# A Mamba block with a routed feed-forward on one core: the sort's counts taken on TensorE, two result buffers, and a new order of the work

## The chip, the core and the metric

The kernel runs on one core of a Trainium2 chip. The metric is the device time of one execution in microseconds (us). The kernel before was timed three times; the median is 2396.81 us.

## The reference

```python
x = x + mamba(layernorm(x))        # x: (8, 1024, 256) f32
    # mamba(x): xn = layernorm*g+b; u,z = split(xn @ W_in.T)   d_inner 512
    #   u = silu(conv4(u)+b);  dt,B,C = split(u @ W_xp.T)      16+16+16
    #   dt = softplus(dt @ W_dt.T + b_dt);  A = -exp(A_log)
    #   h = exp(dt*A)*h + (dt*u)*B;  y = sum_n h*C  + u*D      16 states
    #   return x + (y * silu(z)) @ W_out.T
x = x + moe(layernorm(x))
    # moe(x): logits = x @ router_w + router_b;  top 2 of 8 experts
    #   weights = softmax of the two logits; tokens sorted by expert
    #   out[token] += w * ((silu(x@gate_e) * (x@up_e)) @ down_e)
```

All is float32.

## The kernel before, in words

**Batches, slots, units.** The 8192 tokens are cut into NQ = 16 batches of T = 512. The scan over one batch is UN = 16 units: a unit is 32 channels x 4 states on the 128 partitions, J = 4 times over, 512 steps each. Time is laid out in slots. Each engine runs one Python loop over the slots and issues in each slot, in a fixed order, what falls there: unit s of the scan in slot s (batch q = s // 16, n = s % 16), besides it pieces of the front of the batches to come and of the tail of the batches before. The engines are tied by semaphores alone, so the order within a slot is the order of the queue and says nothing of time.

**One unit.** GpSimd's *drive* (L1301) writes the scan's input for four groups in one product; ScalarE's *decay* (L945) four exponentials; VectorE (L1089 to L1111) scans groups 0 and 1, multiplies both by C, scans 3, scans 2, multiplies 2; GpSimd's *weigh* (L1309) multiplies group 3; TensorE's *weigh* (L692) sums the states into `yps`. The buffer `hs` has three places, so the drive of unit u waits for TensorE's weigh of unit u-3 (`s_ymm`). GpSimd's slot s is: drive of unit s+1, other pieces, weigh of unit s.

**The front of a batch** is made on TensorE in one PSUM bank, `ring`: X (transposes), U and Z (in-projection), W (convolution), P (x-projection), D (dt), and for the tail O0, O1 (out-projection), F0, F1 (transposes), R0 (router), K0 (ranks). The tables MAKES (TensorE) and TAKES (ScalarE) give for each the slot, counted from the batch's first unit, and a place 0 to 4 within it. Since all but the first share one bank, a piece is made only when ScalarE has taken the piece made before it (`BEFORE`). SU and SZ are silu; D is followed by E (exponential, then two sums) on ScalarE, *round_off* (L1313) on GpSimd, L (logarithm, L886), then *less_lost*, *plus_relu* and *dtu* (L1319, L1324, L1329), which make softplus(dt) and dt*u; `pieces` gives their slots.

**The tail of a batch.** In slot 2 of the next batch VectorE takes the moments of the new x (L1062), GpSimd their deviation (L1273), ScalarE the normalised rows. In slot 7 `route` picks the top two experts (`gap` L1131, `hot` L1135), TensorE's `ranks` counts, for each token, the tokens before it with the same expert, and in slot 8 `weights` and `place` compute each token's row in a sorted copy in HBM. `scatter` (L1339) writes the rows there by indirect DMA from slot 8, one piece of 128 a slot (two a slot in the last two batches). Tiles of 128 sorted rows of one expert then pass through gate, up and down (`tile_transpose`, `gate_up`, `activate`, `down`) at the slots of TILE_AT; ScalarE copies the result into `yt` (L986), and `add_rows` (L1349) adds it into the output by an indirect DMA with addition, one at a time: each waits for the one before (`s_add`). The last batch has LAST = 22 tiles, placed TAIL_AT slots after its end; the tiles from slot LATE_FROM on (8 of batch 14 and these 22) run after the scan and take their weights from the arena.

**place() before.** `r5` holds the counts that `ranks` left in PSUM: for each of four groups of tokens the rank within the batch, and the batch's totals. `state[0]` is the next free row of each expert, `state[1]` the number of rows not yet given to a tile. 22 small VectorE instructions, most of which wait for the one before by `s_place`, form the positions, count full tiles, spread them over the batch's eight tile slots and leave `te` (expert) and `tb` (first row) for SyncE to load by.

## Time and profile before

| | us |
|---|---|
| three runs | 2390.99, 2396.81, 2398.17 |
| profiled execution, its own time | 2390.97 |
| its span | 2389.1 |
| granted TensorE clock, mean | 0.87 of full |
| VectorE busy | 1987.7 |
| GpSimd busy | 1957.3 |
| first drive starts | 75.5 |
| last drive starts | 2199.5 |

The span is from the first to the last instruction of the profiled execution; its time is 1.9 us more. Busy time is the time in which an engine runs an instruction, without its waits. The first and last drive mark where the scan begins and ends: before them lies the front of the first batch, behind them the tail.

### The profile page before, as it was taken

Reading aid. Unit: us, or ns where it says so; the run is one execution under the profiler, and the core shown is the slowest. Engines: PE = TensorE matmul, PEld = TensorE weight load, DVE = VectorE, ACT = ScalarE, POOL = GpSimd, SP = SyncE. Lnnn points to the kernel's source line nnn. Section 1 sums busy time; section 2 is a strip of 40 time slices with the busy share of each in tenths; the row PEclk is TensorE's granted clock in tenths of the full one; section 3 lists DMA queues with packets and bytes.
Section 4 is the critical chain, followed back from the end, with each engine's and each line's share of the span. In section 5 each row is a group of like instructions: output and inputs, shape, how many; then the busy total and the mean of one; then the engine's idle time right before and its main releaser. Section 6 shows DMA issues by size and latency. Waiting matters only on the chain.

```text
span 2389.1 us, 32277 instructions
## 1 busy us (share of the span) xinstructions
PE 1805.6 (76%) x7630; PEld 934.7 (39%) x7630; DVE 1987.7 (83%) x2756; ACT 1719.3 (72%) x3273; POOL 1957.3 (82%) x1284
## 2 busy tenths in 40 slices
PE   6557777686868788787968888786878878665885
PEld 2113222243434444443534444443534444243542
DVE  0499989999898989899898989999898989999311
ACT  5778677877887777877887677877878678754232
POOL 2688787979989897998989898998979898997333
PEclk9789788798989888897989889898989889777998
DMA  2545354575767676685758576686757667597332
GB/s 73 132 103 128 87 140 102 151 185 144 199 152 188 154 188 147 175 198 146 188 147 196 151 190 167 163 202 154 194 137 188 161 176 175 156 249 225 77 59 35
DMA packets 217979, 369.34 MB, mean 155 GB/s; under 512 B 31040, under 2 KB 86592, under 8 KB 217664
## 3 DMA queue, kind: packets, MB, share of 16 engines
q1 hardware_dynamic: 192208, 333.56, 54.0%
q0 software_dynamic: 25584, 33.71, 7.2%
q8 instruction: 65, 1.06, 0.2%
q14 instruction: 122, 1.00, 0.1%
HBM read 285.05 MB, written 83.01 MB: 154 GB/s over the span
## 4 chain that ended last, share of the span: by engine, by line
PE 35%; POOL 20%; issue 17%; ACT 16%; DVE 7%; DMA 4%; POOLq 0%; ACTq 0%; DVEq 0%
POOL arena L1301 7%; PE yps L692 5%; PE ring L594 4%; PE ring L602 4%; DMA out<-yt,xt 4%; PE p_g L724 4%; ACT dA L945 4%; DVE dA L1089 4%; PE ring L622 3%; POOL sorted_x L1339 3%; POOL arena L1309 2%; PE ring L610 2%; POOL out L1349 2%; POOL rst L1273 2%; PE p_a L704 2%
## 5 line engine op out<-in xcount | busy, mean ns | idle before, releaser
L1301 POOL TENSOR_TENSOR arena<-arena,b_bc 128x2048 f32<-128x2048 f32 x256 | 985.3, 3849 | 67.6 <-PE yps L692 63.7
L945 ACT ACTIVATE dA<-arena,a_s 128x512 f32<-128x512 f32 x1024 | 673.1, 683 | 135.7 <-DVE arena L1098 106.2
L1089 DVE TENSOR_TENSOR_SCAN dA<-dA,arena 128x512 f32<-128x512 f32 x384 | 454.7, 1215 | 137.7 <-ACT dA L945 103.1
L1089 DVE TENSOR_TENSOR_SCAN dA<-dA,carry,arena 128x512 f32<-128x512 f32 x384 | 477.8, 1275 | 39.2 <-POOL arena L1301 23.3
L692 PE MATMUL yps<-arena,const_s 128*32 128x512 f32 x2048 | 325.6, 712 | 210.8 <-POOL arena L1309 135.0
L1098 DVE TENSOR_TENSOR arena<-dA,c_bc 128x1024 f32<-128x1024 f32 x256 | 313.6, 1225 | 8.8
L1349 POOL DMA_INDIRECT out<-yt,xt x135 | 215.5, 1597 | 115.6 <-DMA out<-yt,xt 62.0
L1309 POOL TENSOR_TENSOR arena<-arena,c_bc 128x511 f32<-128x511 f32 (+1 forms) x256 | 296.0, 1156 | 15.7 <-DVE arena L1089 14.8
L594 PE MATMUL ring<-arena 128*128 128x512 f32 x488 | 258.6, 656 | 58.5 <-ACT arena L853 34.3
L724 PEld LDWEIGHTS p_g<-xT,w_e 128*128 128x128 f32 x1680 | 230.7, 215 | 28.9 <-issue 26.1
L724 PE MATMUL p_g<-xT,w_e 128*128 128x128 f32 x1680 | 236.1, 300 | 6.5 <-DVE hT L1222 6.5
L602 PE MATMUL ring<-arena 128*128 128x512 f32 x480 | 221.0, 603 | 19.9 <-ACT xn_t L928 9.6
L692 PEld LDWEIGHTS yps<-arena,const_s 128*32 128x32 f32 x2048 | 45.0, 117 | 395.2 <-issue 285.2
L1111 DVE TENSOR_TENSOR arena<-dA,c_bc 128x512 f32<-128x512 f32 x256 | 177.1, 692 | 8.3
L1339 POOL DMA_INDIRECT sorted_x<-xf,pos x128 | 128.0, 1000 | 47.1 <-issue 24.3
L1089 DVE TENSOR_TENSOR_SCAN arena<-dA,carry,arena 128x512 f32<-128x512 f32 x128 | 163.3, 1275 | 0.0
L594 PEld LDWEIGHTS ring<-arena 128*128 128x128 f32 x488 | 92.9, 207 | 171.1 <-issue 77.1
L1089 DVE TENSOR_TENSOR_SCAN arena<-dA,arena 128x512 f32<-128x512 f32 x128 | 155.3, 1214 | 0.3 <-ACT dA L945 0.3
L704 PE MATMUL p_a<-w_e,hT 128*128 128x256 f32 x420 | 146.3, 480 | 0.5 <-ACT xT L978 0.5
L1319 POOL TENSOR_TENSOR arena<-arena,t_s 128x512 f32<-128x512 f32 x64 | 80.6, 1260 | 70.9 <-ACT arena L886 70.5
L704 PEld LDWEIGHTS p_a<-w_e,hT 128*128 128x128 f32 x420 | 87.9, 232 | 129.9 <-issue 114.2
L602 PEld LDWEIGHTS ring<-arena 128*128 128x128 f32 x480 | 87.1, 191 | 122.3 <-issue 88.7
(165 smaller groups left out, 2967.6 us busy)
## 6 DMA issues: line engine op xcount, KB each, us to landing
arena<-dt_d SPq DMA_DIRECT2D x512, 256.0 KB
w_e<-in_w_moe SPq DMA_DIRECT2D x105, 512.0 KB
dt_d<-arena SPq DMA_DIRECT2D x128, 256.0 KB, 2.3
w_e<-in_w_moe SPq DMA_DIRECT2D x105, 256.0 KB
xt<-sorted_x SPq DMA_DIRECT2D x135, 129.0 KB
b_bc<-bc_d SPq DMA_DIRECT2D x256, 64.0 KB, 2.1
c_bc<-bc_d SPq DMA_DIRECT2D x256, 64.0 KB
xs<-in_x SPq DMA_DIRECT2D x16, 512.0 KB, 6.9
```

The source lines that it names most:

```text
L594: last = pe.matmul(bank(q, name), w_in_s[:, c, ch * P:(ch + 1) * P], xnT[:, c, :], start=c == 0, stop=c == DC - 1)
L602: last = pe.matmul(bank(q, f"W{c}"), d_conv[:, c, k, :], ubuf[:, c % 2, k:k + T], start=k == 0, stop=k == TAPS - 1)
L692: last = pe.matmul(yps[32 * j:32 * j + 32, :], sumsel, hs[:, u % 3, j, :], start=False, stop=g == G - 1, skip_group_check=True)
L704: last = pe.matmul(p_a[:, DM:2 * DM], hT[:, v % 2, c, :], w_e[:, v % 2, col:col + DM], start=c == 0, stop=c == DC - 1)
L724: last = pe.matmul(p_g[:, f, :], w_e[:, v % 2, col:col + P], xT[:, v % 2, c, :], start=c == 0, stop=c == DC - 1)
L945: act.activation(dA[:, j, :], rep_dt[:, c % 2, j, :], ACT.Exp, scale=a_s[:, n, j:j + 1]).then_inc(s_exp, 1)
L1089: return dve.tensor_tensor_scan(out_ap, dA[:, j, :], hs[:, u % 3, j, :], init, ALU.mult, ALU.add)
L1098: dve.tensor_tensor(hs[:, u % 3, 0:2], dA[:, 0:2], c_bc[:, g, :].unsqueeze(1).to_broadcast([P, 2, T]), ALU.mult).then_inc(s_m01, 1)
L1301: pool.tensor_tensor(hs[:, u % 3], rep_dtu[:, c % 2], b_bc[:, g, :].unsqueeze(1).to_broadcast([P, J, T]), ALU.mult).then_inc(s_dbu, 1)
L1309: pool.tensor_tensor(hs[:, u % 3, 3, 0:end], hs[:, u % 3, 3, 0:end], c_bc[:, g, 0:end], ALU.mult).then_inc(s_hp, 1)
L1339: pool.indirect_dma_start(out=sorted_x, out_offset=bass.IndirectOffsetOnAxis(ap=pos[:, q % 2, k, t:t + 1], axis=0), in_=xf[:, q % 2, t, :] ...
L1349: pool.indirect_dma_start(out=out_rows, out_offset=bass.IndirectOffsetOnAxis(ap=number, axis=0), in_=yt[:, v % NY, :], in_offset=None, bou ...
```

## The change

It has four parts.

1. `ranks` gets the running state into the sum on TensorE: two matmuls with the identity add `r5[:, QT]` (next free row) to all five rows and `r5[:, QT+1]` (rows not given out) to a sixth, and the counting matmuls run over one row more. `state` and `row` are gone: `r5` is [P, 6, 8] and is both the state and the new table. ScalarE's copy of it waits for `s_state` in place of `s_pos`.
2. `place` has 18 instructions for 22. `count_e`, `upto`, `some`, `base`, `step` and `past` are one or two columns wider, with borders set once at the start (three more memsets); the shifted copy of `upto`, the clipping of `te` and the last addition of `base` and row numbers are gone; `full` has a buffer of its own.
3. `yt` has two buffers for three (NY).
4. The order: MAKES, TAKES, `pieces`, `ahead`, the order of the calls in each engine's slot, SyncE's too, scatters two a slot for all batches, TAIL_AT 15 for 19.

```diff
-LG, PL, WT = 2, 16, 3
-NX, NY = 7, 3
+LG, PL, WT = 2, 13, 3
+NX, NY = 7, 2
-TAIL_AT = 19
+TAIL_AT = 15
-        a_slot = 2 if q >= NQ - 2 else 1
+        a_slot = 2 if q >= NQ - 2 else 2
...
 MAKES (slots and places that the prediction speaks of)
-  (-15,3) U2  (-14,2) U3  (-11,4) P0  (-10,4) D0  (-9,0) Z0  (-8,0) Z1
-  (16,4) O0   (17,4) O1   (1,0) D3    (21,1) R0   (23,2) K0
+  (-14,1) U2  (-14,4) U3  (-10,0) P0  (-10,2) D0  (-9,2) Z0  (-9,3) Z1
+  (16,3) O0   (17,1) O1   (1,0) D3    (21,2) R0   (23,3) K0
 TAKES
-  (-10,4) D0,E0  (-8,0) Z1,L0  (-3,2) L1  (0,3) L2  (17,0) O0  (23,3) K0
+  (-10,4) D0  (-9,0) E0  (-8,0) Z1,L0  (-3,2) L1  (0,0) L2  (17,2) O0  (24,0) K0
...
             def ranks(q):
+                pe.wait_ge(s_tables, 5)
+                wait(pe, s_state, q)
+                rows = ring[:, 0:(n + 2) * NE].rearrange("p (i e) -> p i e", e=NE)
+                pe.matmul(rows[:, 0:n + 1], ident, r5[:, n:n + 1, :].to_broadcast([P, n + 1, NE]), start=True, ...)
+                pe.matmul(rows[:, n + 1:n + 2], ident, r5[:, n + 1:n + 2, :], start=False, ...)
                 for k in range(2):
-                    pe.matmul(ring[:, 0:n * NE], before, hot[:, k, 0:n, :], start=k == 0, ...)
+                    pe.matmul(rows[:, 0:n], before, hot[:, k, 0:n, :], start=False, ...)
                     for i in range(n):
-                        later = n - i
+                        later = n + 1 - i
...
 TensorE's slot: weigh(s - 1) goes behind down, late_down and late_turn
 ScalarE's slot
-  keep01, decay 1, gap_exp, decay 0, second_weight, take 0, norm_x, decay 3, take 1, take 2, keep2,
-  norm_x2, take_y, take 3, decay 2, take_y (late), take 4, late_take, keep3, tanh, take_xt
+  second_weight, take 0, keep01, decay 0, norm_x, decay 1, decay 3, take 1, late_take, gap_exp, take 2,
+  norm_x2, keep2, keep3, take_y (late), take 3, take 4, decay 2, take_xt, tanh, take_y
 VectorE's slot: moments(0) first and a slot earlier, activate ahead of route
 GpSimd's slot
-  drive, add_rows, scatter, less_lost, plus_relu, dtu, deviation(0), round_off, weigh, deviation(1)
+  drive, deviation(0), add_rows, scatter, less_lost, weigh, deviation(1), plus_relu, dtu, round_off
-  plus_relu (-8, -2, 1, 3)  dtu (-7, -1, 1, 4)  round_off (-9, -3, -1, 2)
+  plus_relu (-8, -2, 0, 4)  dtu (-8, -2, 0, 4)  round_off (-9, -4, -1, 1)
 SyncE's slot
-  load_tile, store_bc (n 9), load_down, store_x2 (4), load_x (6), load_late, load_c, load_b,
-  store_dt (-6, -1, 2, 5), load_rep, load_expert
+  store_x2 (n 5), load_x (5), load_b, store_bc (6), load_down, load_tile, load_late,
+  store_dt (-5, 0, 3, 7), load_expert, load_rep, load_c
...
             def place(q):
-                a = row = r5[0:QT] + state[0]
-                c = row2 = hot * row
-                b = state += r5[QT]
-                d = full = state[1] >= 128, 256, ...
+                a = row2 = hot * r5[0:QT]
+                b = full = r5[QT + 1] >= 128, 256, ...
                 posf, count_e, pos, head, upto (scan)
-                past; upto[1] = upto[0] - count_e; base; some; step; tef; taken; past *= step
-                state[1] -= 128 * taken; tbf; te = min(tef, 7); tbf += base[0] + rows; tb = min(tbf, ZERO_PAGE)
+                past; base; some; step; tef; taken; past *= step
+                r5[QT + 1] -= 128 * taken; te = tef; tbf; tb = min(tbf, ZERO_PAGE)
```

In the tables, the two slot orders and `place` the diff is written out in short; a slot such as (-8, 0) is counted from the first unit of the batch, and 16 more or less is the same slot of a neighbouring batch.

## Rows read from the trace of the kernel before

**Rows 1.** The page: busy time by engine, and the chain by engine.
```profile
PE 1805.6 (76%) x7630; PEld 934.7 (39%) x7630; DVE 1987.7 (83%) x2756; ACT 1719.3 (72%) x3273; POOL 1957.3 (82%) x1284
...
PE 35%; POOL 20%; issue 17%; ACT 16%; DVE 7%; DMA 4%; POOLq 0%; ACTq 0%; DVEq 0%
```

**Rows 2.** Stretches: length, busy PE, PEld, DVE, ACT, POOL; PEclk, DMA share, GB/s.
```profile
75.50:2199.50 2124.00, 1627.04 (x7014) 833.43 (x7013) 1934.23 (x2608) 1621.22 (x3045) 1874.62 (x1198) 0.87 0.65 164
...
1140.00:1274.20 134.20, 107.59 (x497) 57.43 (x490) 121.41 (x171) 110.84 (x231) 121.63 (x79) 0.90 0.69 173
```

**Rows 3.** Waits of VectorE, 75 to 2199 us: us in total, times, longest.
```profile
DVE dA L1089 <- POOL arena L1301: 57.6, 64, 2.1
DVE stats L1062 <- ACT xs L924: 37.6, 14, 2.8
```

**Rows 4.** Waits of GpSimd, the same stretch.
```profile
POOL arena L1319 <- ACT arena L886: 69.6, 21, 6.2
POOL arena L1301 <- PE yps L692: 63.7, 21, 5.2
```

**Rows 5.** VectorE in time, batch 8, unit 2: start us, us, instruction, idle before.
```profile
1155.84 2.35 DVE L1089 TENSOR_TENSOR_SCAN dA<-dA,arena 128x512 f32<-128x512 f32 x2 [0.34 <-POOL arena L1301]
...
1162.29 0.69 DVE L1111 TENSOR_TENSOR arena<-dA,c_bc 128x512 f32<-128x512 f32 x1
1165.78 1.41 DVE L1062 BATCH_NORM_STATS2 stats<-xs 128x6 f32<-128x256 f32 x4 [2.80 <-ACT xs L924]
...
1167.52 2.31 DVE L1089 TENSOR_TENSOR_SCAN dA<-dA,arena 128x512 f32<-128x512 f32 x2
```

**Rows 6.** TensorE in time: the begin of O1; the begin of ranks.
```profile
1160.46 1.99 PE L622 MATMUL ring<-w_out_s,sz 128*128 128x256 f32 x8 [0.92 <-ACT arena L853]
...
1207.14 0.41 PE L647 MATMUL ring<-hot,const_s 128*128 128x32 f32 x2 [0.84 <-ACT sz L862]
```

**Rows 7.** ScalarE in time, batch 8, slots 7 and 8.
```profile
1209.58 0.20 ACT L934 ACTIVATE r<-ring 128x40 f32<-128x40 f32 x1 [2.07 <-PE ring L650]
...
1213.86 1.28 ACT L886 ACT_TABLE_LOAD   x1
1215.15 0.63 ACT L886 ACTIVATE arena<-arena 128x512 f32<-128x512 f32 x1
```

**Rows 8.** VectorE in time: the first and the last instruction of place().
```profile
1210.62 0.19 DVE L1167 TENSOR_TENSOR row<-r,state 128x32 f32<-128x32 f32 x1
...
1213.77 0.17 DVE L1210 TENSOR_SCALAR tb<-tbf 128x8 uint32<-128x8 f32 x1
```

**Rows 9.** GpSimd in time, batch 8: drive 8; slot 8.
```profile
1199.38 3.81 POOL L1301 TENSOR_TENSOR arena<-arena,b_bc 128x2048 f32<-128x2048 f32 x1 [3.45 <-PE yps L692]
...
1212.14 1.01 POOL L1339 DMA_INDIRECT sorted_x<-xf,pos  x1 [0.74 <-DVE pos L1182]
1215.86 1.08 POOL L1319 TENSOR_TENSOR arena<-arena,t_s 128x512 f32<-128x512 f32 x1 [2.71 <-ACT arena L886]
```

**Rows 10.** GpSimd's groups in batch 8: plus_relu and dtu; busy, mean ns, idle before.
```profile
L1324 POOL TENSOR_TENSOR arena<-arena 128x512 f32<-128x512 f32 x4 | 5.7, 1421 | 0.2
...
L1329 POOL TENSOR_TENSOR arena<-arena,uc 128x512 f32<-128x512 f32 x4 | 4.4, 1094 | 0.1
```

**Rows 11.** GpSimd in time: the first and the last of 22 additions.
```profile
2288.42 1.54 POOL L1349 DMA_INDIRECT out<-yt,xt  x1 [3.23 <-DMA out<-yt,xt]
...
2381.69 1.55 POOL L1349 DMA_INDIRECT out<-yt,xt  x1 [2.00 <-DMA out<-yt,xt]
```

**Rows 12.** Line 1131: shortest, median, longest ns; first and last start.
```profile
L1131 DVE TENSOR_TENSOR gap<-mx x16: 166/711/3484, 264.7 to 2247.4; 128x4 f32<-128x4 f32 x16
```

**Rows 13.** VectorE in time: line 1131 beside unit 7 of batches 8 and 15.
```profile
1203.80 1.08 DVE L1131 TENSOR_TENSOR gap<-mx 128x4 f32<-128x4 f32 x1
...
2147.34 3.48 DVE L1131 TENSOR_TENSOR gap<-mx 128x4 f32<-128x4 f32 x1
```

**Rows 14.** GpSimd in time, the same.
```profile
2147.00 3.81 POOL L1301 TENSOR_TENSOR arena<-arena,b_bc 128x2048 f32<-128x2048 f32 x1
```

More of the change, by code:

```diff
@@ L63, in __init__ @@
         elif q == NQ - 2:
-            self.at = [self.ready + k for k in [18, 20, 21, 22, 23, 25, 26, 28]]
+            self.at = [self.ready + k for k in [18, 20, 21, 22, 23, 25, 26, 29]]
         else:
@@ L261, in mamba_moe @@
         hot = sb("hot", [P, 2, QT, NE])
-        r5 = sb("r5", [P, QT + 1, NE])
-        state = sb("state", [P, 2, NE])
-        row = sb("row", [P, QT, NE])
+        r5 = sb("r5", [P, QT + 2, NE])
         row2 = sb("row2", [P, 2, QT, NE])
@@ L559, in _ @@
                         load_b(0, g)
-                for p, k in pieces(s, (-6, -1, 2, 5), (-10, -1, 3, 5)):
+                if q >= 0 and front and n == 6 or s == -13:
+                    store_bc(q + 1)
+                for g, k in tiles_in(s - 1, False):
+                    load_down(g, k)
+                for g, k in tiles_in(s + 1):
+                    load_tile(g, k)
+                if q == NQ - 1 and n in (4, 5, 6, 7, 9, 10, 13, 14):
+                    load_late((4, 5, 6, 7, 9, 10, 13, 14).index(n))
+                for p, k in pieces(s, (-5, 0, 3, 7), (-10, -1, 3, 7)):
                     store_dt(p, k)
+                for g, k in tiles_in(s + 1, False):
+                    load_expert(g, k)
                 if 0 <= q < NQ and n in (0, 4, 8):
@@ L575, in _ @@
                             no_tokens(e)
+                if n == 0 and 0 <= q < NQ:
+                    load_c(q, G - 1)
+                if front and n >= 13:
+                    load_c(q + 1, n - 13)
             sp.wait_ge(s_add, 16 * TILES)
@@ new lines, in place @@
+                h = step_of(dve.tensor_scalar(some[:], upto[:], float(nk), None, ALU.min))
+                dve.wait_ge(s_place, g5)
+                i = step_of(dve.tensor_tensor(step[:, 0:NE + 1], base[:, 1:NE + 2], base[:, 0:NE + 1], ALU.subtract))
+                dve.wait_ge(s_place, f)
+                dve.tensor_reduce(tef[:, 0:nk], past[:, 0:nk, 1:NE], AX_X, ALU.add).then_inc(s_past, 1)
+                dve.wait_ge(s_place, h)
+                j = step_of(dve.tensor_tensor(taken[:], some[:, 1:NE + 1], some[:, 0:NE], ALU.subtract))
@@ L1227, in _ @@
                 tail = 0 <= q - 1 < NQ
+                for p in ahead(s, 9, -21):
+                    moments(0, p)
                 if unit:
@@ L1237, in _ @@
                     unit_second(s)
+                for g, k in tiles_in(s - 2):
+                    activate(g, k)
                 if n == 7 and tail:
@@ L1243, in _ @@
                     moments(1, q - 1)
-                for p in ahead(s, 10, -21):
-                    moments(0, p)
                 if unit and n in (4, 8, 12):
@@ L1361, in _ @@
                     drive(s + 1)
+                for p in ahead(s, 11, -20):
+                    deviation(0, p)
                 for g, k in tiles_in(s - 4, False):
@@ L1369, in _ @@
                     less_lost(p, k)
-                for p, k in pieces(s, (-8, -2, 1, 3), (-11, -1, 1, 3)):
-                    plus_relu(p, k)
-                for p, k in pieces(s, (-7, -1, 1, 4), (-11, -1, 1, 4)):
-                    dtu(p, k)
-                for p in ahead(s, 11, -20):
-                    deviation(0, p)
-                for p, k in pieces(s, (-9, -3, -1, 2), (-12, -3, 0, 2)):
-                    round_off(p, k)
-                if s == UN * (NQ - 1) + 5:
-                    no_token()
                 if 0 <= s < UN * NQ:
@@ L1383, in _ @@
                     deviation(1, q - 1)
+                for p, k in pieces(s, (-8, -2, 0, 4), (-11, -1, 1, 4)):
+                    plus_relu(p, k)
+                if s == UN * (NQ - 1) + 6:
+                    no_token()
+                for p, k in pieces(s, (-8, -2, 0, 4), (-11, -1, 1, 4)):
+                    dtu(p, k)
+                for p, k in pieces(s, (-9, -4, -1, 1), (-12, -3, 0, 1)):
+                    round_off(p, k)
 def program(nc, args):
```

177 lines of the change are left out of this document (76 added, 101 removed), and 25 rows, old and new, of tables (MAKES, MAKES0, TAKES, TAKES0).

## The prediction

> **What bounds the kernel now.** I read the page's busy line and chain first [rows 1]. The reader is to see that no engine holds the path: VectorE is busy 83% of the span and GpSimd 82%, and the chain goes through all four. The stretches [rows 2] say where the time lies: 2124 of 2389 us between the first and the last drive of the scan's 256 units. In one batch (16 units, 134.2 us) VectorE works 121.4 us and GpSimd 121.6 us, so each is idle 12 to 13 us and neither can be sped up alone. The waits say at whose door this idle time lies. VectorE loses 57.6 us to GpSimd's drive and 37.6 us in 14 waits of the second layernorm's moments for ScalarE's copy of the out-projection [rows 3]. GpSimd loses 69.6 us to ScalarE's logarithm and 63.7 us to TensorE's weigh, which frees the buffer of the drive [rows 4].
>
> Within a batch the two take turns, which the timelines of batch 8 show. Unit 2 begins the moment its drive is there (0.34 us late) and unit 3 only 11.68 us later, where the moments sat idle for 2.80 us [rows 5]. In slots 4 to 8 GpSimd has little to do and waits for others; in slot 8 it waits 2.71 us for the logarithm, and ahead of drive 8 it waited 3.45 us for TensorE's weigh [rows 9]. From there to the next slot 2 it has no idle time to speak of, and VectorE follows it. So a batch is: GpSimd from the logarithm of slot 8 to drive 2, then VectorE from unit 2 to unit 8.
>
> **The change part by part.** The sum is made against the profiled execution (span 2389.1 us, its time 2391.0 us); the median of the runs is 5.8 us above it, and I add these at the end.
>
> 1. *Out-projection in slot 17, the moments' wait.* Before, O1 is made at place 4, behind U2: only when ScalarE has copied U2 (line 853), at 1160.46, can O1 begin; it lasts 4.6 us, so it ends when VectorE has long been done with unit 2 [rows 5, 6]. After, U2 is gone to slot 18 and O1 stands right behind D3. Against this, O0 is taken later in ScalarE's slot (place 2 for place 0), about 1.1 us, and D3 and O1 with it: O0 copied 1155.0, D3 made and taken 1157.4, O1 ends 1162.0, its copy 1162.7 (hand reckoning with the same durations), while unit 2 itself keeps VectorE until 1162.98. The wait goes whole. What is late next is drive 3: GpSimd has 9.0 us of work between drives 2 and 3 (a row addition, plus_relu, dtu, weigh, drive), and VectorE's unit 2 without the stall has 8.9, which would cover almost the whole gain at units 3 and 4 if nothing else moved. But plus_relu and dtu of slot 1 (1.42 + 1.09 us [rows 10]) go to slot 0, ahead of drive 2, so drive 3 is no longer in the way. Value: 14 waits, 37.6 us [rows 3], of which I take 36. Bounds 0 and 37.6.
>
> 2. *GpSimd's order and the scatters in pairs.* Its work in a batch stays as it is; it only moves. In front of the logarithm's wait in slot 8 there now stand two scatters for one: 1.0 us and a gap of 0.2 [rows 9] leave the loaded stretch. The logarithm itself comes earlier: ScalarE now takes K0, Z1 and L0 ahead of its own decays, so it waits for TensorE's ranks (end about 1210.0), Z1 (1.8 us), the copy, the table load and the logarithm (0.5 + 1.28 + 0.63 [rows 7]), about 1214.7 where it was 1215.8, 1.1 us. Against these two, the 2.5 us of plus_relu and dtu now ahead of drive 2. Net for drive 2: +0.2 us a batch, taken as 0. Bounds over 14 batches: -32 us (if the two pieces fill time that is idle) to +34 us (if neither of the gains comes).
>
> 3. *place(), 18 small steps for 22.* It runs from 1210.62 to 1213.94 [rows 8], 3.3 us, 0.15 each; the wider tables (10 columns for 8) cost little on steps that take 0.16 to 0.28 us. So 0.6 us less. But GpSimd is then still waiting for the logarithm, until 1215.86 [rows 9], and VectorE falls in behind GpSimd from unit 12 on. Value 0, cover: the logarithm's wait; without this cover -0.6 x 15 = -9 us.
>
> 4. *ranks() with two identity matmuls more, taken a place later.* Ten matmuls run from 1207.14 to the copy at 1209.58 [rows 6, 7], 0.24 each, so +0.5 us. A gate_up of 1.9 us now stands ahead of it, but that one is ready while ranks still waits for the copy of Z0. The table copy comes at 1210.1 to 1210.3 and place() begins at 1210.6: value 0. Bound: if gate_up does push it, (0.5 + 1.9 - 0.8) x 15 = +24 us. Its wait for the state of the batch before is long satisfied.
>
> 5. *ScalarE's decays.* Decay 0 now comes before 1, the order in which the scans use them, and the takes of place 0 stand ahead of them, in time where ScalarE waits for VectorE's first product. Value 0; bounds -9 to +9 us (0.6 us, one exponential, a batch).
>
> 6. *Two result buffers.* The copy of result v now waits for addition v-2 and not v-3. The additions wait for one another anyway: 22 of the tail start from 2288.42 to 2381.69, 4.44 us apart [rows 11], and the copy has the flight of one whole addition to hide in. Value 0; if it fell between them, 30 x 0.5 = +15 us. Behind the waiting copy ScalarE has the next tiles' copies and tanh, which the same 4.4 us cover.
>
> 7. *The tail, TAIL_AT 15.* The slots in between are empty, so an earlier number starts nothing earlier. The last tile's turn now stands behind the first transposes of the new tiles and waits for their load, but its addition is due only 9 us later. Value 0, except that K0 goes behind a gate_up here with nothing to hide it: +1.9 + 0.5 - 0.6 (place) = about +1.5 us on the first scatter and so on the row of additions. Bounds -2 and +5.
>
> 8. *SyncE's order, earlier moments, three more memsets.* SyncE blocks longer in slot 5 (store of x, then the load that needs it), store_dt goes up to two slots later. Its data are wanted three slots later, 24 us. Value 0, bounds 0 and +10.
>
> Sum: 2391.0 - 36 + 1.5 = 2356.5; with 5.8 us on top, 2362 us.
>
> **The rivals.** (A) *GpSimd keeps what VectorE gains* (same side or none). The pieces bunched in slots 8, 14 and 0, with pairs of scatters in 8 to 11, make drives 9 to 15 and 1, 2 late. For it: VectorE already loses 57.6 us to the drive [rows 3]. Against: the sum of its work is the same. Price: the +34 us of part 2, so 2396 us.
>
> (B) *A drive catches the router's small steps* (slower). The step that makes `gap` reads two tensors from SBUF and takes 166 ns alone, but 711 in the median and 3484 at most [rows 12]. That one case shows why: the drive began at 2147.00 and lasted 3.81 us [rows 14], the step began at 2147.34 and ended with it [rows 13]. In the other batches a short piece (round_off or weigh) stood there, the step waited for its end and was served ahead of the drive. The change puts weigh ahead of round_off in slot 7, so now the drive can follow a short piece that ends before `hot` is asked for. It decides at one point: is drive 9 begun before `hot`? If so, `hot`, the ranks, place() and the logarithm are all about 3.3 us later (3.48 - 0.17), 15 times, +50 us: 2362 + 50 = 2412 us. Against it, in batch 8: drive 8 ends at 1203.2 [rows 9], weigh and round_off (1.1 each) at 1205.4; `gap`, asked for at 1203.80 [rows 13], would wait only for weigh, to 1204.3, and with 0.7 us for itself and the index steps `hot` is asked for at 1205.0, 0.4 us ahead of the drive.
>
> The Trainium skill, page "SBUF — State Buffer", section "Who interferes with whom", says that a VectorE instruction with two SBUF inputs contends with a GpSimd one that reads SBUF, and that whoever issues first makes the other wait for the whole instruction; by that rule this rival holds at each such meeting, and the one long step of the trace agrees with it.
>
> (C) *The idle time of GpSimd goes as well* (faster still). If part 2 comes in at its lower bound and place() counts: -32 - 9, 2321 us. For it: 69.6 and 63.7 us of waits [rows 4], which the new order of the takes aims straight at. Against: the waits in slot 8 hang on VectorE, which is itself full there.
>
> **How the numbers follow.** My forecast 0.52, (A) 0.13, (B) 0.17, (C) 0.18. The forecast's own range is 2345 to 2380 us; the whole range goes to (C) and most of (B): 2321 to 2406 us. What a measurement of this kernel can tell from no change is about 0.3%, 7 us. Faster by more: 0.52 + 0.18 and a little of (A), 0.71. Within: most of (A), 0.10. Slower: (B) and the ends of parts 4 to 8, 0.19.
>
> **What would show it.** Part 1: the wait of the moments' statistics for the copy goes from 37.6 us to under 5, and unit 2 of a batch lasts about 9 us. Part 2: the wait for the logarithm falls from 69.6 us toward 45, VectorE's wait for the drive stays near 57.6. Part 3: place() lasts 2.7 us. Part 4: its wait for the table copy stays under 5 us in all. Part 6: additions in the tail 4.4 us apart. A batch takes 132 us and not 134 to 135. (B) shows as a median of `gap` or `hot` over 2 us. The forecast is wrong if VectorE's waits for the drive grow by as much as the moments' wait shrinks, or if the tail after the last drive (190 us) changes by more than 5 us.

## The result, and the profile after

The kernel after takes 2409.74 us (median of 5 runs, 2407.51 to 2411.09), the kernel before, beside it, 2397.61 us (5 runs, 2390.99 to 2400.09). The ratio is 1.005, 95% interval 1.0033 to 1.0066: 12 us slower, where 2362 us had been forecast. The profiled execution of after has a span of 2407.8 us and a time of 2409.8.

The page of the kernel after: busy time by engine, and the chain by engine.
```profile
PE 1834.8 (76%) x7694; PEld 949.2 (39%) x7694; DVE 1964.2 (82%) x2693; ACT 1716.3 (71%) x3273; POOL 1955.1 (81%) x1287
...
PE 29%; POOL 21%; issue 19%; DVE 13%; ACT 13%; DMA 4%; POOLq 0%; DVEq 0%; ACTq 0%
```
Against [rows 1] VectorE has 23.5 us less to do and GpSimd about the same (2.2 us less), yet the span grew, so what grew on these two is waiting. TensorE is busy 29.2 us more, at a mean granted clock of 0.857 of full for 0.869.

The stretch from the first to the last drive; the columns are those of [rows 2].
```profile
77.33:2213.84 2136.51, 1647.71 (x7065) 844.21 (x7065) 1911.97 (x2549) 1616.27 (x3044) 1872.17 (x1197) 0.85 0.66 163
```
It is 12.5 us longer than in [rows 2]. The rest of the 18.7 us between the two spans is 1.8 ahead of it and 4.4 behind it. (The profiled execution of before is 6.6 us under its median; that is why the spans differ by more than the 12 us of the medians.) Cut by the first scan of each batch, batches 0 and 1 take 254.0 us for 242.8, batches 2 to 14 take 135.30 us each for 134.94.

The waits of VectorE in the kernel after, 75 to 2205 us (us in total, times, longest).
```profile
DVE dA L1094 <- ACT dA L949: 139.5, 66, 73.3
DVE dA L1094 <- POOL arena L1301: 58.2, 58, 1.9
DVE sz L1121 <- PE yps L696: 37.6, 13, 3.9
DVE row L1172 <- ACT r L938: 15.2, 14, 1.2
...
DVE stats L1066 <- ACT xs L928: 2.5, 3, 0.9
```
The last row is the gain that was forecast: the moments waited 37.6 us [rows 3] and now wait 2.5. But 37.6 us at the gating (line 1121) are new (5.5 before), the wait for ScalarE's decays grew from 112.5 to 139.5, and that of place() for the table from 2.3 to 15.2. The longest wait for the decays, 72.2 us before and 73.3 after, is the one ahead of the first unit and stands in both totals.

The waits of GpSimd, and one of TensorE, in the same stretch.
```profile
POOL arena L1301 <- PE yps L696: 81.9, 33, 5.3
POOL arena L1319 <- ACT arena L890: 42.4, 16, 5.4
```
```profile
PE p_a L708 <- ACT xT L982: 136.1, 28, 7.8
```
The logarithm is waited for less (42.4 for 69.6 [rows 4]), TensorE's weigh more (81.9 for 63.7). The row of TensorE has next to no counterpart before (0.5 us): the product with w_down (line 708) waits 136 us for ScalarE to copy the transposed tile, because both use the buffer p_a. In return weigh itself waits less, 93.2 us for GpSimd and 16.3 for ScalarE where it was 135.0 and 74.2, so most of this idle time has only moved. What matters is what stands behind the product, and batch 8 shows it.

TensorE in time in the kernel after, unit 6 and 7 of a batch: start us, us, instruction, idle time before it.
```profile
1214.24 1.10 PE L708 MATMUL p_a<-w_e,hT 128*128 128x256 f32 x4 [2.33 <-ACT xT L982]
1215.28 1.07 PE L696 MATMUL yps<-arena,const_s 128*32 128x512 f32 x8
1216.27 1.98 PE L594 MATMUL ring<-arena 128*128 128x512 f32 x4
1218.09 1.95 PE L728 MATMUL p_g<-xT,w_e 128*128 128x128 f32 x16
1219.88 0.31 PE L649 MATMUL ring<-r,const_s 128*128 128x40 f32 x2
```
ScalarE in the same time.
```profile
1213.11 0.69 ACT L949 ACTIVATE dA<-arena,a_s 128x512 f32<-128x512 f32 x1
1213.72 0.38 ACT L982 ACTIVATE xT<-p_a 128x256 f32<-128x256 f32 x1
```
TensorE is idle 2.33 us until ScalarE, behind its last decay, has made the copy. Behind that product stands weigh (line 696), which GpSimd's next drive needs, and behind that ranks (line 649), which begins 2.7 us after the end of `hot` in the tail of every batch from 2 to 12.

### The profile page after: what moved, and what is told of

It is laid out like the page before. It is cut to its first block, busy times and chain, and to the rows that moved or that the text cites. A ratio compares the mean times of both kernels' runs of the same rounds, so it can differ in the third digit from the quotient of the medians.

```text
span 2407.8 us, 32361 instructions
## 1 busy us (share of the span) xinstructions
PE 1834.8 (76%) x7694; PEld 949.2 (39%) x7694; DVE 1964.2 (82%) x2693; ACT 1716.3 (71%) x3273; POOL 1955.1 (81%) x1287
## 3 DMA queue, kind: packets, MB, share of 16 engines
q8 instruction: 65, 1.06, 0.2%
## 4 chain that ended last, share of the span: by engine, by line
PE 29%; POOL 21%; issue 19%; DVE 13%; ACT 13%; DMA 4%; POOLq 0%; DVEq 0%; ACTq 0%
POOL arena L1301 8%; DVE dA L1094 8%; PE ring L594 5%; PE yps L696 4%; DMA out<-yt,xt 4%; PE ring L602 4%; ACT dA L949 3%; POOL sorted_x L1339 2%; POOL out L1349 2%; PE p_g L728 2%; POOL arena L1309 2%; PE p_a L708 2%; POOL arena L1324 2%; DVE arena L1094 2%; PE ring L610 2%
## 5 line engine op out<-in xcount | busy, mean ns | idle before, releaser
L1301 POOL TENSOR_TENSOR arena<-arena,b_bc 128x2048 f32<-128x2048 f32 x256 | 1000.3, 3907 | 86.8 <-PE yps L696 82.3
L949 ACT ACTIVATE dA<-arena,a_s 128x512 f32<-128x512 f32 x1024 | 664.7, 680 | 131.8 <-DVE arena L1103 95.1
L696 PE MATMUL yps<-arena,const_s 128*32 128x512 f32 x2048 | 308.7, 677 | 109.6 <-POOL arena L1309 93.2
L1309 POOL TENSOR_TENSOR arena<-arena,c_bc 128x511 f32<-128x511 f32 (+1 forms) x256 | 346.8, 1355 | 15.1 <-DVE arena L1094 14.0
L594 PE MATMUL ring<-arena 128*128 128x512 f32 x488 | 297.4, 741 | 71.5 <-ACT sz L866 48.0
L602 PE MATMUL ring<-arena 128*128 128x512 f32 x480 | 261.2, 694 | 20.2 <-ACT xn_t L932 9.6
L728 PEld LDWEIGHTS p_g<-xT,w_e 128*128 128x128 f32 x1680 | 213.1, 204 | 74.0 <-issue 74.0
L728 PE MATMUL p_g<-xT,w_e 128*128 128x128 f32 x1680 | 225.4, 291 | 7.7 <-DVE hT L1219 7.7
L708 PEld LDWEIGHTS p_a<-w_e,hT 128*128 128x128 f32 x420 | 98.9, 244 | 216.1 <-issue 197.8
L594 PEld LDWEIGHTS ring<-arena 128*128 128x128 f32 x488 | 97.0, 220 | 203.8 <-issue 97.2
L602 PEld LDWEIGHTS ring<-arena 128*128 128x128 f32 x480 | 100.3, 220 | 155.1 <-issue 108.3
L622 PE MATMUL ring<-w_out_s,sz 128*128 128x256 f32 x512 | 124.2, 386 | 13.8 <-ACT uc L861 12.7
```

The source lines that it names most:

```text
L594: last = pe.matmul(bank(q, name), w_in_s[:, c, ch * P:(ch + 1) * P], xnT[:, c, :], start=c == 0, stop=c == DC - 1)
L602: last = pe.matmul(bank(q, f"W{c}"), d_conv[:, c, k, :], ubuf[:, c % 2, k:k + T], start=k == 0, stop=k == TAPS - 1)
L696: last = pe.matmul(yps[32 * j:32 * j + 32, :], sumsel, hs[:, u % 3, j, :], start=False, stop=g == G - 1, skip_group_check=True)
L708: last = pe.matmul(p_a[:, DM:2 * DM], hT[:, v % 2, c, :], w_e[:, v % 2, col:col + DM], start=c == 0, stop=c == DC - 1)
L728: last = pe.matmul(p_g[:, f, :], w_e[:, v % 2, col:col + P], xT[:, v % 2, c, :], start=c == 0, stop=c == DC - 1)
L949: act.activation(dA[:, j, :], rep_dt[:, c % 2, j, :], ACT.Exp, scale=a_s[:, n, j:j + 1]).then_inc(s_exp, 1)
```

## The experiments

Each kernel ran beside the kernel before on its chip; a ratio is to that one, with its 95% interval. One per cent is 24 us.

**1. Weigh ahead of the product with w_down again.** The kernel after with
```
                 for item in made_in(s, 0):
                     make(item)
+                if 0 < s <= UN * NQ:
+                    weigh(s - 1)
                 for g, k in tiles_in(s - 3, False):
                     down(g, k)
...
-                if 0 < s <= UN * NQ:
-                    weigh(s - 1)
```


> The kernel after, with TensorE's weigh again ahead of down. Theory W: down waits for ScalarE's copy of a later tile (136 us, 28 times, 7.8 at most) and the weigh behind it comes late, so the drives wait for it (81.9 us before the last drive, 63.7 in the kernel before). Then the drives' wait falls by about 20 us and the time by 10 to 20 us, to 2390 to 2400 us. Theory P: the drives that wait for the weigh stand in slot 8 and 15, where GpSimd is ahead anyway, so nothing changes: 2405 to 2412 us.

Measured: 2384.61 us (2378.8 to 2387.7), ratio 0.9952 [0.9933, 0.9971], 24 us under the kernel after. The waits, GpSimd's and TensorE's:
```profile
POOL arena L1301 <- PE yps L696: 48.3, 29, 4.9
POOL arena L1319 <- ACT arena L890: 37.0, 17, 3.6
```
```profile
PE p_a L708 <- ACT xT L982: 16.4, 14, 1.3
```
All that the order of TensorE had brought is gone: the 136 us, a part of GpSimd's wait, and VectorE's wait for the decays is 111.9 us, as before. That order is one cause; theory W had it, at 10 to 20 us. TensorE stands idle as long as before, now at weigh, for GpSimd (219.1 us for 93.2): the product was late for a copy that weigh doesn't need. The new 37.6 us at the gating stay (43.1).

**2. One scatter a slot.** The kernel after, then (second) the kernel of experiment 1 with second_weight moved behind two decays as well, and (third) the kernel before with pairs.
```
-        a_slot = 2 if q >= NQ - 2 else 2
+        a_slot = 2 if q >= NQ - 2 else 1
```


> The kernel after, with the scatters of batches 0 to 13 again one a slot (slots 8 to 15). Theory P (pairs): the pairs put three more scatters (3.9 us) between the logarithm of slot 8 and drive 13, on an engine that has no idle time there, and VectorE, which waits for those drives, cannot make it up later, since from unit 13 on its own work sets the pace. Then this kernel wins back most of the 4.1 us that units 8 to 12 lost, less the 1.3 us given back behind them: 2 to 3 us a batch, 28 to 40 us, so 2370 to 2382 us, and the wait of gated for TensorE's weigh (37.6 us) falls under 10. Theory W (TensorE's weigh behind down) and theory S (ScalarE's takes ahead of the decays) expect no change, 2405 to 2412 us.

> x2_weigh_first with the scatters of batches 0 to 13 one a slot, and second_weight behind the decays 0 and 1, as in the kernel before (in x1 ScalarE stood 49.0 us, 14 times 3.5, in front of second_weight for the scatter to land, ahead of the decays). Theory P (the pairs hold drives 10 to 13 late and VectorE can't make it up): 20 to 40 us faster than x2, 2345 to 2365 us, and the wait of gated in slot 12 (43.1 us) goes. If GpSimd's order within the batch doesn't matter: 2380 to 2388 us.

> The kernel before with one edit: the scatters of all batches two a slot. Theory P: 25 to 40 us slower than before, 2422 to 2437 us, in units 9 to 13, with GpSimd's deviation in slot 11 behind a pair. If the pairs hurt only together with the other edits (W, S), within 7 us of before.

Measured: 2467.95 us, ratio 1.03 [1.0278, 1.0323]; second 2395.1 us, 0.9974 [0.9956, 0.9993]; third 2402.06 us, 1.004 [1.0023, 1.0057]. The first is so slow for another reason than the scatters. Its ScalarE, the waits (75 to 2260 us):
```profile
ACT xf L975 <- DMA sorted_x<-xf,pos: 44.6, 13, 6.8
```
second_weight now stands ahead of all decays, and with this step it asks for a scatter that has not landed; VectorE's wait for the decays rose to 222.8 us. That this wait makes up the 60 us is read from these rows; second_weight was moved back only in the second kernel, together with weigh. There, one scatter a slot gives 0.9974 for 0.9952: 5 us, which is within the noise of the two, and not the 20 to 40 us faster that theory P asked for. In the old order pairs cost 10 us, where theory P asked for 25 to 40. The pairs bring the wait at the gating, as VectorE's waits in the third kernel show:
```profile
DVE sz L1116 <- PE yps L692: 46.6, 18, 3.5
```
In the second it is 9.4 us. Whether it counts is experiment 7.

**3. GpSimd waits for `hot` ahead of the drive of slot 8.** The kernel of experiment 1 with
```
+                if n == 8 and 1 <= q < NQ:
+                    pool.wait_ge(s_hot, q)
                 if 0 <= s + 1 < UN * NQ:
                     drive(s + 1)
```


> x2_weigh_first, and GpSimd's drive of unit 9 (slot 8) waits for s_hot, so that it can't begin ahead of `hot`. In x2 `hot` lasts 3.23 us in 8 of 15 batches, always when the drive began first. Theory H (a VectorE step with two SBUF inputs stands still while the drive reads SBUF, and the step is on the path): each of these steps falls to 0.2 to 0.9 us and 8 x 2.7 us, some 20 us, come off: 2360 to 2370 us. If the step is not on the path, or the drive's own delay eats it, 2380 to 2388 us as x2.

Measured: 2346.59 us (2339.17 to 2347.81), ratio 0.9762 [0.9738, 0.9786]: 46 us under experiment 1 by the ratios (38 by the medians), and under both kernels. Theory H had asked for some 20. First the kernel of experiment 1, in time, VectorE's `hot`, GpSimd's drive and the last part of ranks:
```profile
1338.30 3.81 POOL L1301 TENSOR_TENSOR arena<-arena,b_bc 128x2048 f32<-128x2048 f32 x1
...
1338.95 3.24 DVE L1140 TENSOR_TENSOR hot<-ix,const_s 128x64 f32<-128x64 uint32 x1
...
1344.07 1.87 PE L655 MATMUL ring<-hot,const_s 128*128 128x40 f32 x8
```
The drive began 0.65 us ahead of `hot`, and `hot` ended 0.08 us behind it. Over the 16 batches (line 1140 in both: shortest, median, longest in ns; of experiment 1, and of this kernel):
```profile
L1140 DVE TENSOR_TENSOR hot<-ix,const_s x16: 224/3236/3239, 269.0 to 2240.2; 128x64 f32<-128x64 uint32 x16
```
```profile
L1140 DVE TENSOR_TENSOR hot<-ix,const_s x16: 224/227/842, 270.9 to 2202.8; 128x64 f32<-128x64 uint32 x16
```
The same place with the wait:
```profile
1319.86 0.23 DVE L1140 TENSOR_TENSOR hot<-ix,const_s 128x64 f32<-128x64 uint32 x1
1320.16 3.81 POOL L1301 TENSOR_TENSOR arena<-arena,b_bc 128x2048 f32<-128x2048 f32 x1 [0.91 <-DVE hot L1140]
...
1322.53 1.04 PE L655 MATMUL ring<-hot,const_s 128*128 128x40 f32 x8
```
GpSimd stands 0.91 us and VectorE wins 3.01. In the kernel of experiment 1 `hot` was caught in 9 of 15 tails, 8 of them of the batches 2 to 14, and the `gap` of batch 14 too (3.48 us). The 13 batches 2 to 14 are 33 us shorter in sum with the wait.

A catch costs more than its own 3 us. Behind the late `hot` TensorE had been idle for 2.2 us. The second half of ranks then took 1.87 us for 1.04, and the piece Z1 behind it, which ScalarE takes right ahead of the logarithm, 3.78 us in each of the eight, for 1.98 in nine of the twelve comparable batches with the wait. The columns are those of [rows 2], experiment 1 in the second half of ranks, and then this kernel over most of them:
```profile
1344.00:1346.00 2.00, 1.94 (x10) 1.83 (x10) 1.97 (x2) 0.26 (x2) 0.98 (x1) 0.52 1.06 273
```
```profile
1321.00:1323.00 2.00, 2.00 (x21) 2.00 (x20) 2.00 (x2) 1.14 (x3) 2.00 (x1) 1.00 1.07 223
```
TensorE was granted half its clock in the first and all of it in the second. In batch 8, whose unit 7 runs alike in both kernels up to `hot`, less_lost (which needs the logarithm) starts 21.32 us behind the begin of unit 7 with the catch and 16.25 without, and unit 13 58.98 and 53.84: 5.1 us, of which 3.0 are `hot` (in batch 9 it is 4.1). Eight of these come to 33 to 41 us, and 38 were measured by the medians. Rival (B)'s mechanism is shown, by removing it; the part of the clock is read from the rows and was not tried apart.

**4. The same wait alone**, in the kernel after and in the kernel before.

> The kernel after with one line added: GpSimd waits for `hot` ahead of the drive of slot 8; TensorE's weigh stays behind the product with w_down. Nothing else is changed. Theory C (a drive that catches `hot` costs time at each meeting, whatever the rest of the order): in the trace of the kernel after, `hot` lasted 3.24 us in 3 of 15 batches only, so the wait has 3 x 2.5 us to win here: -8 us, about 2402 us, ratio to before near 1.002. Rival J (the gain of the run with both edits, 38 us for 8 long steps, was more than the steps' own 20 us; it comes from the drive standing behind `hot` as such, which gives VectorE's router a free port in all batches): -25 us or more, under 2385 us, ratio below 0.995. Under theory C `hot` is never above 0.9 us in the profile and TensorE's wait for ScalarE's copy of the tile stays above 100 us.

> The kernel before with the same line alone: GpSimd waits for `hot` ahead of the drive of slot 8. Before, `gap` and `hot` last 0.5 to 1.5 us and not 3.3: they are served between two short pieces. Theory C: there is no meeting with a whole drive to remove here, and the drive would start up to 0.5 us later; same, ratio 0.998 to 1.002 (2395 to 2405 us). Rival J: 15 us or more faster, ratio below 0.994.

Measured: 2394.8 us, ratio 0.9984 [0.9961, 1.0007], 16 us under the kernel after; and 2390.82 us, ratio 0.998 [0.9958, 1.0002]. Rival J falls: where no drive catches `hot`, the wait gives nothing that can be told. In the kernel after it won more than the 8 us that theory C gave it (9 us between the two spans); it removed the catches in the tails of batches 0, 1 and 13 (`hot`) and 14 (`gap`), and in those of 4 to 12 `hot` and ranks stand where they stood, to 0.1 us from the start of unit 7. Alone the two mends give 16 and 24 us, together 69. That is the key to the case: with TensorE's late weigh, drive 8 waits 3.8 us for it, and the drive behind it begins only when `hot` has been asked for.
```profile
1210.89 3.81 POOL L1301 TENSOR_TENSOR arena<-arena,b_bc 128x2048 f32<-128x2048 f32 x1 [3.81 <-PE yps L696]
...
1217.06 3.81 POOL L1301 TENSOR_TENSOR arena<-arena,b_bc 128x2048 f32<-128x2048 f32 x1
```
```profile
1216.36 0.83 DVE L1140 TENSOR_TENSOR hot<-ix,const_s 128x64 f32<-128x64 uint32 x1
```
Those are the drives and the `hot` of batch 8 in the kernel after: `hot` waits for GpSimd's short round_off (1216.02 to 1217.11) and is served ahead of the drive. Over the tails of batches 0 to 13 of this kernel and that of experiment 1 it goes by the start of drive 8, counted from the start of unit 7: `hot` is caught where that is 0.65 or 1.06 us, and never where it is 1.65 us or more. Mending the first cause brought in the second.

**5. The sort and the two buffers.** The kernel before with the new ranks, place() and two result buffers (with three there was no room); with two buffers alone; the first of these with GpSimd's wait; and the kernel of experiment 3 with the old sort.
```
-        NX, NY = 7, 3
+        NX, NY = 7, 2
```


> The kernel before with the new ranks and place alone (and two result buffers, which make room for the wider tables); the whole old order. The prediction costed the shorter place at 0 because GpSimd still waits for the logarithm: 2392 to 2402 us. If place is on VectorE's path in slot 8, the 0.8 us that it is shorter (3.3 before, 2.5 after) come off in each of 15 batches: 12 us, 2385 us. If two result buffers cost something, it shows here as a time over 2402 us.

> The kernel before with two result buffers in place of three, nothing else. It splits the run of the sort alone (+22 us), which needed the two buffers for the room of its tables. Theory S (the sort's order costs: the ranks take 2.75 us for 2.4 and the small steps meet more of GpSimd): the buffers cost nothing, ratio 0.999 to 1.002, and the sort has the whole 22 us. Rival N (the copy of a result waits for the row addition two before, in the batches as in the tail): +5 to +20 us, ratio 1.002 to 1.009, with ScalarE's or GpSimd's waits at the row additions larger and additions of the tail more than 4.5 us apart.

> The kernel with the new sort and the two result buffers alone (the run that gave 1.0087) with GpSimd's wait for `hot` ahead of the drive of slot 8. Theory M (the sort is slower because its steps meet GpSimd's drive more often: `hot` 1.1 us in the mean against 0.7): some 10 to 20 us come back, ratio 1.000 to 1.005. Rival R (it is slower because two more matmuls and the table from TensorE put the whole chain ranks, copy, place, logarithm later): the wait brings nothing, ratio 1.007 to 1.010, and GpSimd's wait for the logarithm stays near 90 us.

> The fastest kernel so far (weigh ahead of the product with w_down, GpSimd waits for `hot`; 0.9762 of before) with the sort of before put back: ranks of 10 matmuls, the running counts added on VectorE, 22 small steps. The two result buffers and every order stay. Theory K (once the router's steps meet no whole drive, the sort still costs by its longer chain; beside the old order it cost 0.1%, 3 us, with the wait and 0.9% without): 0 to 10 us faster than that kernel, ratio 0.972 to 0.976, place() 3.3 us, ranks 2.4 us. Rival P (its shorter place() counts once VectorE is the bound): 5 to 15 us slower, ratio 0.978 to 0.982.

Measured: 2415.46 us, 1.0087 [1.0055, 1.0118]; 2399.28 us, 1.0005 [0.9982, 1.0028]; 2404.78 us, 1.0014 [0.9991, 1.0036]; 2341.65 us, 0.9761 [0.9735, 0.9786]. The buffers cost nothing that can be told. The sort cost 21 us in the old order, of which the wait gives 17 back (some 9 more or less). But no `hot` was caught by a drive there: it fell only from 0.80 to 0.72 us in the mean and `gap` from 0.97 to 0.59, half of that by the one `gap` of batch 14. What stayed in both is longer ranks: 3.80 us in the median, for 2.40 before, and only 0.35 of that is the longer sum (2.75 in the kernel after). In the tail of batch 8 the granted clock is 0.50 over the second half of ranks in the sort-only kernel and 1.00 before. So the cause of the 21 us is not settled. GpSimd's wait for the logarithm in the sort-only kernel:
```profile
POOL arena L1318 <- ACT arena L889: 91.0, 21, 6.3
```
It was 69.6 [rows 4], and is 85.1 with the wait, so rival R has a share. In the new order the sort is worth 0 +- 8 us, though place() takes 2.48 us for 3.32 and GpSimd's first scatters wait less for its positions (10.8 us for 21.0 with the old sort).

**6. Part 1 and part 2 taken apart.** The kernel before with U2 and O1 moved as in the change (first). The kernel of experiment 3 with GpSimd's plus_relu and dtu put back, slots and order (second: both calls right behind less_lost, ahead of weigh), and slots alone (third):
```
                 if 0 <= s < UN * NQ:
                     weigh(s)
...
-                for p, k in pieces(s, (-8, -2, 0, 4), (-11, -1, 1, 4)):
+                for p, k in pieces(s, (-8, -2, 1, 3), (-11, -1, 1, 3)):
                     plus_relu(p, k)
...
-                for p, k in pieces(s, (-8, -2, 0, 4), (-11, -1, 1, 4)):
+                for p, k in pieces(s, (-7, -1, 1, 4), (-11, -1, 1, 4)):
                     dtu(p, k)
```


> The kernel before with one move: U2 made in slot 18 (place 1, taken at place 2) and O1 in slot 17 at place 1, behind D3. It takes away the moments' wait of 37.6 us. The prediction took 36 us for this move together with the new order of GpSimd's pieces; alone, with 9.0 us of GpSimd's work between drives 2 and 3, it expects next to nothing: 2388 to 2395 us. If VectorE's wait was the path: 2358 to 2370 us.

> The same fastest kernel with GpSimd's plus_relu and dtu put back to where they stood before: slots 1 and 3, and 1 and 4, right behind less_lost and ahead of weigh, in place of slots 0 and 4 behind weigh. Theory G (the moments' 37 us are won only because drive 3 comes in time: moving O1 alone won nothing, unit 3 grew from 7.3 to 10.0 us, and these two pieces of 2.5 us were what stood ahead of drive 3): 20 to 35 us slower, ratio 0.984 to 0.991, unit 3 of a batch over 9 us and VectorE's wait for the drive over 60 us. Rival D (moving O1 alone failed because ScalarE's takes then bunched ahead of its decays, and GpSimd's pieces don't matter): within 8 us, ratio 0.973 to 0.980.

> The fastest kernel of the first runs (0.9762 of before) with GpSimd's plus_relu and dtu in the slots of before (1 and 3, 1 and 4, for 0 and 4), but behind weigh, as there, and not ahead of it. The run with the old slots and the old order ahead of weigh gave 1.0004: 55 us slower. Theory O (the order ahead of weigh is what costs: 2.5 us ahead of TensorE's product in up to four slots of a batch, GpSimd's wait for it 91 us for 50): within 12 us of the fastest, ratio 0.976 to 0.981, GpSimd's wait for weigh under 60 us. Rival L (the slot is what costs: with the two pieces in slot 1 drive 3 is late when unit 2 ends early): ratio over 0.990, GpSimd's wait for weigh small, VectorE's wait for the drive over 65 us.

Measured: 2407.15 us, 1.0017 [0.9988, 1.0046]; 2401.84 us, 1.0004 [0.9984, 1.0023]; 2387.01 us, 0.9944 [0.992, 0.9968]. O1 alone gives nothing that can be told: the moments' wait falls to 5.2 us, but unit 3 grows from 7.3 to 10.0 us and the wait for the decays from 112.5 to 147.8. A drive caught `hot` in three tails of its trace (3.24 us each) and in none before, so some 10 us of a gain may be hidden there. Undoing GpSimd's move costs 58 us; the slot alone costs 44 of them, so rival L has most of it and theory O a quarter, and theory G's price (20 to 35) was too low. Their signs came only in part: VectorE's wait for the drive is 50.7 us in the third kernel, where rival L had said over 65, and 46.6 in the second, where theory G had said over 60. Unit 3 is not what grows (7.2, where G had said over 9); the time stands at the end of unit 2 (10.97 us for 8.69) and in unit 4 (8.23 for 7.20). GpSimd and VectorE in time, third kernel, slot 1:
```profile
1558.74 1.86 POOL L1324 TENSOR_TENSOR arena<-arena 128x512 f32<-128x512 f32 x1
...
1560.68 1.09 POOL L1329 TENSOR_TENSOR arena<-arena,uc 128x512 f32<-128x512 f32 x1
1561.73 1.09 POOL L1313 TENSOR_TENSOR t_s<-t_s,arena 128x512 f32<-128x512 f32 x1
...
1562.77 3.81 POOL L1301 TENSOR_TENSOR arena<-arena,b_bc 128x2048 f32<-128x2048 f32 x1
...
1566.67 2.47 DVE L1094 TENSOR_TENSOR_SCAN dA<-dA,carry,arena 128x512 f32<-128x512 f32 x2 [1.35 <-issue]
```
The two pieces stand ahead of drive 3, and unit 3 begins 0.09 us after that drive's end, 1.35 us late, though the profile names no releaser. The order ahead of weigh costs the other 14 us; GpSimd's waits in the second kernel (75 to 2250 us):
```profile
POOL arena L1301 <- PE yps L696: 91.2, 35, 5.4
```
It is 50.1 in experiment 3 and 66.8 in the third kernel.

**7. The gating of slot 12, and K0 ahead of gate_up.** The kernel of experiment 3 with the third gating behind the first product of slot 13; and the kernel of experiment 1 with K0 made in the place before (23, 2), Z0 likewise.
```
+                if unit and n == 13:
+                    gated(q, 2)
                 if unit:
                     unit_third(s)
...
-                if unit and n in (4, 8, 12):
+                if unit and n in (4, 8):
```


> The fastest kernel of the first runs with one piece of VectorE moved: the third gating of a batch (the product of TensorE's sum with sz) stands no longer at the end of slot 12, where it waits 43.4 us in all for TensorE's weigh of unit 11, but behind the first product of slot 13, some 3.6 us later. Theory V (VectorE itself is the bound there and the 2.9 us a batch are lost to nobody else): the wait goes and 20 to 40 us with it, ratio 0.960 to 0.968. Rival T (TensorE's weigh of unit 12 needs the buffer that the gating frees, and GpSimd's drive needs that weigh, so the lateness comes back as a wait for the drive): within 8 us, ratio 0.973 to 0.980, GpSimd's wait for weigh up by 20 us or more.

> x2_weigh_first with the ranks made at place 2 of slot 7 and taken at place 3 of slot 7, ahead of gate_up, as before (Z0 back at place 0). Theory: ranks' later place costs place() its wait (15.2 us in the kernel after, 3.6 in x2) and the logarithm its start; then 0 to 10 us faster than x2. If `hot` is what comes last, no change, 2380 to 2388 us.

Measured: 2343.84 us, 0.9755 [0.9731, 0.9778]; and 2455.86 us, 1.0223 [1.0199, 1.0247]. The first is the same as experiment 3, though its wait at the gating fell from 43.4 to 1.2 us. The time came back at the scans: VectorE's wait for the drive is 59.9 us for 43.3, and what the profile gives to no releaser is 41.7 for 9.6. VectorE and GpSimd in time:
```profile
1366.84 2.47 DVE L1094 TENSOR_TENSOR_SCAN dA<-dA,carry,arena 128x512 f32<-128x512 f32 x2 [4.68 <-issue]
```
```profile
1359.55 1.05 POOL L1341 DMA_INDIRECT sorted_x<-xf,pos  x1 [0.45 <-issue]
1360.90 0.96 POOL L1341 DMA_INDIRECT sorted_x<-xf,pos  x1 [0.30 <-issue]
1361.88 1.10 POOL L1311 TENSOR_TENSOR arena<-arena,c_bc 128x512 f32<-128x512 f32 x1
1362.93 3.82 POOL L1303 TENSOR_TENSOR arena<-arena,b_bc 128x2048 f32<-128x2048 f32 x1
```
Drive 13 ends at 1366.75 and unit 13 starts 0.09 us later. GpSimd, with the deviation and a pair of scatters ahead of that drive, is the bound of that slot, and the gating had only stood in time that was lost anyway. Rival T had the size right and the way wrong: GpSimd's wait for weigh did not grow (50.2). The other kernel is 65 us slower than experiment 1, where 0 to 10 faster had been expected. A drive catches `hot` in 11 of its 15 tails (9 in experiment 1), and what now stands behind ranks pays for it: in batch 8 TensorE is idle 3.80 us ahead of ranks, which then take 5.27 us, and gate_up behind them 3.72 for 1.95, at a granted clock of 0.50. GpSimd's addition of slot 8 waits for ScalarE's result copy, which stands behind tanh and that behind gate_up (27.5 us in experiment 1):
```profile
POOL out L1348 <- ACT yt L989: 111.3, 11, 10.6
```

## Why the prediction was wrong

The forecast was 2362 us, the result 2410, over the top of the range (2406). The kernel with both causes mended takes 2347 us (experiment 3), inside the range and 15 us below the forecast (by the ratio to before, 21). A batch takes 135.3 us where 132 had been said, and 131.0 in experiment 3. The sign that was to show the forecast wrong, VectorE's wait for the drive growing as the moments' wait shrinks, did not come (58.2 us for 57.6): the loss stood elsewhere.

**The step that failed is one that the working did not have.** The change moves weigh on TensorE behind the product with w_down. The prediction costed TensorE's order only in part 4, for the ranks, and left weigh's new place out without a reason. To ask what the product ahead waits for would have shown it: the buffer p_a, held until ScalarE's copy, the last piece but two of a slot. Measured: 24 us, by putting weigh back (experiment 1). The rest of the loss is rival (B), below, at too low a chance.

**Rival (B), 0.17.** Its mechanism was right, its place and size nearly so: `hot`, not `gap`, 3.24 us for 0.23, caught by the drive of unit 9. It named a margin of 0.4 us on hand reckoning, too thin to leave it at 0.17. By its own sign (a median of `hot` over 2 us) it did not happen in the kernel after, where the median is 0.84 us and 3 of 15 tails are caught, since the late weigh held the drive back. So its 2412 us, which lay outside the stated range, meet the 2410 measured by luck. With weigh mended the median is 3.24 and it costs 38 to 46 us against the +50 it was priced at, which is luck too: 9 catches of some 4 to 5 us, where 15 of 3.3 had been taken. The Trainium skill's page "SBUF — State Buffer", section "Who interferes with whom", says that whichever of the two issues first makes the other wait for the whole instruction; the pair 1338.30 and 1338.95 agrees with it to 0.1 us.

**Part 1 (-36 us): right, and conditional.** The wait fell by 35.1 us, unit 2 of a batch lasts 8.6 us (9 were forecast). Moving O1 alone gives nothing, and the working had said why it would come: plus_relu and dtu leave the way of drive 3.

**Part 2 (0; -32 to +34): mis-sized.** The moved pieces carry the gain of part 1: without them 58 us are lost. They were priced by their own 2.5 us a batch (14 times that is 35, not 34) and put at nothing beside, when parts 1 and 2 are one change. The pairs cost nothing that can be told in the new order and bring a wait of 37.6 us that is not on the path. The wait for the logarithm fell to 42.4, as said (toward 45).

**Part 3 (0): right in the new order.** place() takes 2.48 us for 3.32 (2.7 forecast), and the old sort in its place gives the same time, 0.9761 and 0.9762. In the old order the new sort costs 21 us, which the working did not foresee.

**Part 4 (0; to +24): right on the size** (ranks 2.75 us for 2.40, +0.35 where 0.5 was taken); wrong on the wait, 15.2 us where under 5 was said. With weigh mended it is 3.6.

**Part 5 (0)** was not tried apart; the wait for the decays is 111.9 us once weigh is mended, 112.5 before, with the 69 and 72 us ahead of the first unit in them. **Part 6 (0): right**, 1.0005. The additions of the tail are as far apart as before; GpSimd in time, the first and the last of 24, (2400.31 - 2297.88) / 23 = 4.45 us:
```profile
2297.88 1.55 POOL L1349 DMA_INDIRECT out<-yt,xt  x1 [3.85 <-DMA out<-yt,xt]
...
2400.31 1.55 POOL L1349 DMA_INDIRECT out<-yt,xt  x1 [2.00 <-DMA out<-yt,xt]
```
**Part 7 (+1.5; -2 to +5):** the tail behind the last drive is 4.4 us longer, in its bounds; whether the order does it is open, as it is also 4.4 us longer in the kernel before with two result buffers alone, and 1.2 in the sort-only kernel, which has them too (one execution each). **Part 8 (0; to +10):** not tried apart.

**Rival (A)** failed as it was put (drives late by the bunching), and rival (C) was not what happened either, though the mended kernel goes its way: experiment 3 stands 57 us under before where C had 76, and its wait for the logarithm is 26.3 us for 69.6.

**The sum.** In ratios to before: the rest of the change -2.4% (57 us), drives that catch `hot` +1.9% (46), weigh behind the product +1.0% (24): +0.5%, the result. The second of these is what it costs once the third is mended; in the kernel after each hides the other in part. Mended the other way round, the wait for `hot` gives 16 us and weigh then 53.

**Open:** batches 0 and 1 take 254.0 us for 242.8, and still 251.7 in the fastest kernels. With O1 alone moved it is 249.2. With the wait for `hot` in the kernel after it is 251.8, so 2.2 us were catches. The cause of the other 6 to 9 us was not sought. What the sort costs in the old order, and by which step, is not settled either.

## What to carry to other kernels

Before an order written by hand is changed, list for each moved step what every instruction it now stands behind waits for; on in-order engines the wait is inherited, and here it was a PSUM buffer held by another engine's last piece. Two costs can hide each other: mend one and measure again before the other is judged, and test the parts together as well as alone. Where a long GpSimd operation can begin ahead of a tiny VectorE step on the critical chain, one semaphore wait ahead of the long one gives back more than it costs: 0.9 us of GpSimd for 3.0 us of the chain. Where the two do not meet it gave nothing that can be told (0.998).

## What the runs showed of the hardware

A step on 64 elements a lane, 0.23 us alone, took 3.24 us when it was issued 0.65 us behind a GpSimd operation of 3.81 us, and ended 0.08 us behind it. VectorE's products with one input in PSUM (dA) and one in SBUF show no such thing: all 256 of line 1103 took 1224 to 1227 ns in the kernel after, 106 of them wholly within a drive. The same ranks took 2.75 us at one time, 3.7 where TensorE had been idle 2.2 us ahead of them, and 5.27 where it had been idle 3.8 us. In the second case the granted clock was full over their first half (1.00) and half over their second (0.52, 1.87 us for 1.04); in the third it was 0.50 over all of them. A wait of ScalarE for a scatter's landing (3.4 us each, 13 times) stood ahead of all decays in a kernel 60 us slower than the same one without it; no run took the wait alone away.
